# A selective-scan block and expert layer on one core: first state's tiles scaled by ScalarE, one of VectorE's sums kept back between two half scans, and the side work planned anew

## What is computed

```python
def step(h, inp):
    dAi, bxi, ci = inp            # exp(delta*A), delta*B*x, C
    h = dAi * h + bxi             # [b, 512, 16]
    return (h, jnp.einsum('ben,bn->be', h, ci))
...
y = jnp.transpose(ys, (1, 0, 2)) + Dp * x
return y * jax.nn.silu(z)
```

## Time and profile before

| | us |
|---|---|
| median of 3 runs (4428.97 to 4439.7) | 4429.01 |
| the profiled execution's own time | 4429.31 |
| its span | 4428.0 |
| VectorE busy (4736 instructions) | 3814.1, 86% |
| TensorE busy, matmuls | 3599.2, 81% |
| GpSimd busy | 3504.1, 79% |
| ScalarE busy | 3078.4, 70% |

### The profile page before, as it was taken

How to read it: one execution, slowest core, us unless ns; L and a number is a source line. 1 busy time by engine, 2 the same in 40 slices (tenths; PEclk the granted TensorE clock), 3 DMA queues, 4 the chain that set the end, 5 groups by cost and what they waited for, 6 DMA issues and landing times.

```text
span 4428.0 us, 57936 instructions
## 1 busy us (share of the span) xinstructions
PE 3599.2 (81%) x18192; PEld 2560.6 (58%) x18192; DVE 3814.1 (86%) x4736; ACT 3078.4 (70%) x5131; POOL 3504.1 (79%) x2085
## 2 busy tenths in 40 slices
PE   4668596888878888798978888888886988778877
PEld 1444454666556665567555774557654675557656
DVE  3999999998898989989898998989899898989710
ACT  4667576687767777678776886678776787668643
POOL 3898887988878888788887889878787888878611
PEclk7878697899979999899989998899997999889988
DMA  6222242557434674356543674346742575336555
GB/s 195 91 100 101 74 151 83 165 186 227 149 104 149 195 230 134 107 171 222 191 145 111 198 243 153 127 153 193 232 134 98 174 234 185 124 100 213 179 174 176
DMA packets 375804, 705.05 MB, mean 159 GB/s; under 512 B 31937, under 2 KB 205514, under 8 KB 371530
## 3 DMA queue, kind: packets, MB, share of 16 engines
q1 hardware_dynamic: 363210, 667.79, 46.3%
q0 software_dynamic: 12288, 33.57, 2.3%
HBM read 529.82 MB, written 171.44 MB: 158 GB/s over the span
## 4 chain that ended last, share of the span: by engine, by line
DVE 30%; PE 24%; POOL 15%; issue 15%; ACT 11%; DMA 3%; DVEq 0%; SPq 0%; POOLq 0%; ACTq 0%
DVE h L1391 12%; POOL drive L1895 8%; DVE h L1388 7%; DVE y L1405 7%; PE h_t L1165 5%; PE side L1199 4%; PE side L1336 3%; PE side L1328 3%; POOL xs_dram L1970 2%; ACT decay L1610 2%; POOL y L1913 2%; PE side L1227 1%; DMA expert_w<-in_w 1%; POOL drive L1901 1%; POOL work L1982 1%
## 5 line engine op out<-in xcount | busy, mean ns | idle before, releaser
L1895 POOL TENSOR_TENSOR drive<-xu,b_row 128x1024 f32<-128x1024 f32 x960 | 2261.8, 2361 | 396.7 <-DVE h L1391 237.7
L1610 ACT ACTIVATE decay<-delta,neg_a 128x512 f32<-128x512 f32 x2048 | 1400.8, 691 | 800.4 <-DVE h L1391 469.4
L1165 PE MATMUL h_t<-ident,h 128*128 128x128 f32 x8192 | 1339.5, 301 | 525.5 <-DVE y L1405 262.1
L1165 PEld LDWEIGHTS h_t<-ident,h 128*128 128x128 f32 x8192 | 1063.7, 155 | 992.0 <-DVE y L1405 381.7
L1405 DVE SCALAR_TENSOR_TENSOR y<-h_t,c_col,y 128x512 f32<-128x512 f32 x1488 | 1085.2, 729 | 76.3 <-PE h_t L1165 73.9
L1913 POOL TENSOR_TENSOR y<-y,scaled 128x512 f32<-128x512 f32 x496 | 631.4, 1273 | 120.7 <-ACT scaled L1631 119.5
L1391 DVE TENSOR_TENSOR_SCAN h<-decay,drive 128x512 f32<-128x512 f32 x512 | 621.8, 1214 | 64.6 <-ACT decay L1610 36.7
L1391 DVE TENSOR_TENSOR_SCAN h<-decay,h,drive 128x512 f32<-128x512 f32 x512 | 653.6, 1277 | 25.6 <-ACT decay L1610 8.0
L1388 DVE TENSOR_TENSOR_SCAN h<-decay,h,drive 128x512 f32<-128x512 f32 x448 | 572.8, 1279 | 53.2 <-ACT decay L1610 31.4
L1388 DVE TENSOR_TENSOR_SCAN h<-decay,drive 128x512 f32<-128x512 f32 x448 | 544.0, 1214 | 55.2 <-POOL drive L1895 48.5
L1199 PE MATMUL side<-prep_work,conv_diag 128*128 128x512 f32 x960 | 462.9, 607 | 24.2 <-DMA prep_work<-xz_dram 20.3
(11 more groups left out here) (206 smaller groups left out, 4343.8 us busy)
## 6 DMA issues: line engine op xcount, KB each, us to landing
expert_w<-in_w SPq DMA_DIRECT2D x350, 512.0 KB, 4.6
b_row<-b_dram SPq DMA_DIRECT2D x240, 512.0 KB
x_dram<-xu SPq DMA_DIRECT2D x16, 2048.0 KB, 7.6
delta_dram<-prep_work SPq DMA_DIRECT2D x64, 512.0 KB, 3.5
delta<-delta_dram SPq DMA_DIRECT2D x64, 512.0 KB, 4.4
ys_dram<-work SPq DMA_DIRECT2D x40, 512.0 KB, 6.2
work<-xs_dram SPq DMA_DIRECT2D x38, 512.0 KB, 4.9
h<-in_w SPq DMA_DIRECT2D x34, 512.0 KB
```

What stands on the lines that cost most here:

```text
L1165: t = pe.e.transpose(h_t[i % N_H_T][:, c * P:(c + 1) * P], its_h[:, c, :], ident[:, :])
L1610: act.e.activation(decay[:, i % N_DECAY, :], delta[:, c, its], ACT.Exp, scale=neg_a[:, c, w % 2, n:n + 1]).then_inc(decay_made, 1)
L1895: op = pool.e.tensor_tensor(drive[:, k % N_DRIVE, :], xu[:, w % 2, c, :], b_row[:, row % N_B_ROW, :], ALU.mult)
```

## The change

Three things.

1. All eight tiles of the first state of a sample's first direction (`is_first`) go to ScalarE, which scales them straight into `y`; VectorE's `tensor_scalar` is gone.
2. VectorE's sum of an odd tile whose next tile isn't VectorE's (`sum_is_late`) is kept back to the next step, where it stands behind the first half scan of the next unit. The order over four steps becomes: first half, sum, second half, first half, sum, second half, sum.
3. The tables `AT` and `BANK_USE` are other ones: the same 5048 pieces, in other steps and another order of the banks. Some of it: the second token load of sample 1 stands at 2848 (step 178) instead of 1712 (step 107); its four `u_mul` at steps 231 to 244 instead of 174 to 194; `slots` (the routing) of the seventh sample at step 1939 instead of 1916; the expert loads of sample 0, 46 from step 353 to 516 before, have the same ends and stand closer together in the middle; the last entry is step 2225 instead of 2232.

```diff
 AT = {
-    "tok_load": [-2240, -2239, 1456, 1712, 5216, 5600, 9153, 9648, ...
+    "tok_load": [-2240, -2239, 1456, 2848, 5232, 6561, 9202, 10800, ...
...
+        def is_first(i):
+            return i % (2 * TILES) < TB
+
         def by_pool(i):
-            return i % (2 * TB) in POOL_TILES
+            return i % (2 * TB) in POOL_TILES or is_first(i)
+
+        of_vector = list(accumulate(not by_pool(i) for i in range(NW * TILES)))
+        of_pool = list(accumulate(by_pool(i) and not is_first(i) for i in range(NW * TILES)))
 
         def summed_to(i):
-            rounds, into = divmod(i + 1, 2 * TB)
-            return rounds * (2 * TB - len(POOL_TILES)) + into - sum(t < into for t in POOL_TILES)
+            return of_vector[i]
...
         def gathered_to(i):
-            first_rounds, into = divmod(i, 2 * TILES)
-            in_first = [t for t in POOL_TILES if t < TB]
-            return pooled_to(i) - first_rounds * len(in_first) - sum(t <= into for t in in_first)
+            return of_pool[i]
...
+            def sum_is_late(i):
+                return i % 2 == 1 and i + 1 < NW * TILES and by_pool(i + 1)
+
             def sum_tile(i):
...
-                if d == 0 and n == 0:
-                    if b:
-                        dve.wait_ge(y_dumped[tb], 16 * b)
-                    dve.e.tensor_scalar(y[:, tb, :], h_t[i % N_H_T][:, :], c_n, None, ALU.mult).then_inc(summed, 1)
-                else:
-                    wait_y(dve, i)
-                    dve.e.scalar_tensor_tensor(...).then_inc(summed, 1)
+                wait_y(dve, i)
+                dve.e.scalar_tensor_tensor(...).then_inc(summed, 1)
...
                 i = s - 2 * EC
-                if 0 <= i < NW * TILES and not by_pool(i):
-                    sum_tile(i)
+                for its in (i - 1, i):
+                    if 0 <= its < NW * TILES and not by_pool(its) and sum_is_late(its) == (its < i):
+                        sum_tile(its)
...
             def scale_tile(i):
...
-                if d == 0 and n == 0:
+                if is_first(i):
...
-                if 0 <= i < NW * TILES and by_pool(i) and i % (2 * TILES) >= TB:
+                if 0 <= i < NW * TILES and by_pool(i) and not is_first(i):
                     pool_tile(i)
```

More of the change, by code:

```diff
@@ L2 @@
 from contextlib import ExitStack
+from itertools import accumulate
 import concourse.bass as bass
@@ L52 @@
[L52 to L58, removed]
@@ new lines @@
+    "tok_var": [-2160, -2128, 2736, 2912, 5808, 6656, 10352, 10864, 13762, 14240, 18672, 19184, 22017, 22448, 26113,
+        26960, 32992, 33073, 33457, 33584],
+    "neg_a": [-2144],
+    "tok_rstd": [-1952, -1920, 2752, 2928, 6464, 6656, 10720, 10880, 13760, 14368, 18976, 19200, 22016, 22656,
+        26112, 27232, 32992, 33072, 33456, 33584],
+    "tok_apply": [-1920, -1904, -1888, -1856, 2800, 2816, 2960, 2961, 6512, 6528, 6688, 6704, 10736, 10752, 10912,
+        10928, 13808, 13809, 14400, 14402, 19056, 19072, 19232, 19248, 22048, 22064, 22689, 22707, 26144, 26160,
+        27328, 27344, 33008, 33040, 33120, 33121, 33489, 33552, 33616, 33633],
@@ new lines @@
+    "xn_turn": [-1888, -1872, -1840, -1680, 2816, 2832, 2976, 2977, 6560, 6561, 6736, 6737, 10752, 10768, 10960,
+        10976, 13808, 13840, 14416, 14417, 19072, 19088, 19280, 19296, 22080, 22160, 22736, 22753, 26176, 26256,
+        27360, 27376],
+    "cw_make": [-1888, -1808, -1728, -1648, -1536, 160, 288, 416],
+    "xn_copy": [-1872, -1855, -1824, -1663, 2832, 2848, 2976, 2992, 6560, 6576, 6736, 6737, 10784, 10800, 10976,
+        10992, 13840, 13841, 14405, 14416, 19104, 19120, 19296, 19312, 22096, 22208, 22752, 22784, 26192, 26304,
+        27393, 27394],
@@ new lines @@
+    "silu_x": [-1551, -1328, 640, 3488, 4560, 7328, 8688, 11536, 12976, 15008, 17072, 19841, 21232, 23552, 25200,
+        27984, 29552],
+    "dbc_mm": [-1472, -1440, -1280, -1216, 688, 689, 720, 737, 3552, 3568, 3584, 3600, 4768, 4816, 4834, 4864, 7408,
[4 rows of a table added]
+    "dbc_copy": [-1408, -1168, 704, 768, 3616, 3632, 4784, 4880, 7456, 7504, 8752, 8801, 11680, 11696, 13008, 13136,
+        15152, 15536, 17105, 17184, 19984, 20016, 21296, 21424, 23696, 23760, 25266, 25376, 28112, 28304, 29600,
+        29664],
@@ new lines @@
+    "c_turn": [-1392, -1152, 784, 1120, 3680, 3681, 5200, 5201, 7568, 7664, 8850, 9008, 11792, 11808, 13216, 13232,
+        15505, 15905, 17249, 17312, 20064, 20112, 21440, 21473, 24224, 24240, 25408, 25425, 28258, 28384, 29728,
+        29792],
+    "c_copy": [-1376, -1120, 784, 1136, 3680, 3696, 5184, 5200, 7584, 7680, 8848, 9008, 11760, 11792, 13200, 13216,
+        15552, 15904, 17280, 17312, 20080, 20096, 21440, 21472, 24208, 24240, 25408, 25409, 28320, 28400, 29744,
+        29776],
+    "dt_mm": [-1376, -1168, -1120, -1104, -976, -960, -688, -656, 736, 800, 1168, 1184, 1248, 1249, 1344, 1360,
[8 rows of a table added]
@@ new lines @@
+    "softplus": [-1360, -1152, -1088, -1072, -944, -928, -16, 0, 752, 816, 1200, 1232, 1264, 1280, 1360, 1392, 3648,
[8 rows of a table added]
+    "delta": [-1328, -1120, -992, -991, 16, 17, 32, 33, 1120, 1136, 1216, 1248, 1296, 1312, 1376, 1408, 3664, 3680,
[7 rows of a table added]
+    "x_store": [-1280, 672, 3520, 4592, 7361, 8720, 11570, 12976, 15040, 17072, 19873, 21232, 23585, 25232, 28017,
+        29552],
+    "b_store": [-1168, 768, 3633, 4880, 7504, 8801, 11728, 13136, 15568, 17184, 20032, 21456, 23760, 25376, 28336,
+        29664],
@@ new lines @@
+    "top1": [5632, 10192, 14400, 18512, 22656, 26768, 30976, 33713],
+    "rank_mm": [5666, 10209, 14435, 18528, 22688, 26817, 31024, 33776],
+    "mix_turn": [5667, 5696, 10256, 10257, 14436, 14437, 18529, 18576, 22689, 22720, 26818, 26832, 31120, 31136,
+        33792, 33793],
+    "top2": [5648, 10208, 14416, 18528, 22672, 26784, 30992, 33744],
+    "slots": [5664, 10224, 14432, 18544, 22688, 26800, 31024, 33776],
+    "mix_copy": [5680, 5682, 10242, 10243, 14450, 14451, 18560, 18561, 22704, 22706, 26817, 26818, 31136, 31152,
+        33792, 33808],
@@ new lines @@
+    "bias_mm": [5856, 10448, 14992, 18688, 22896, 26960, 31104, 33856],
+    "bias_copy": [5856, 10434, 14992, 18720, 22914, 26992, 31120, 33888],
+    "xs_load": [5904, 5952, 6032, 6112, 6416, 6688, 10480, 10528, 10592, 10704, 11056, 11632, 14672, 14880, 14976,
+        15216, 15488, 15888, 18801, 18864, 18929, 19009, 19312, 19937, 22928, 22993, 23104, 23440, 23856, 24129,
+        27057, 27136, 27202, 27296, 27984, 28256, 31281, 31360, 31440, 31520, 31776, 32064, 34064, 34065, 34128,
+        34193, 34385, 34576],
@@ L431 @@
+    "fin_add": [9056, 9104, 9168, 9184, 13248, 13296, 13360, 13376, 17344, 17360, 17424, 17440, 21504, 21520, 21584,
+        21600, 25552, 25584, 25648, 25712, 29824, 29856, 29888, 29904, 33585, 33600, 33616, 33632, 35504, 35537,
+        35584, 35600],
+    "out_store": [9201, 13393, 17457, 21617, 25729, 29921, 33648, 35552, 35600],
 }
 BANK_USE = {
[L434 to L435 removed]
@@ new lines @@
+    "z_mm": [72, 73, 79, 84, 103, 106, 105, 108, 248, 251, 250, 253, 273, 272, 275, 274, 400, 402, 407, 404, 428,
+        429, 430, 431, 555, 564, 557, 566, 577, 592, 579, 594, 713, 715, 716, 717, 738, 743, 740, 745, 878, 873,
+        880, 875, 898, 895, 900, 897, 1019, 1036, 1021, 1038, 1041, 1064, 1043, 1066, 1078, 1080, 1059, 1082, 1061,
+        1084, 1063, 1073],
+    "y_turn": [91, 96, 95, 100, 110, 114, 113, 118, 265, 264, 267, 266, 277, 276, 279, 278, 417, 420, 422, 421, 432,
+        433, 434, 435, 567, 582, 584, 571, 581, 596, 583, 598, 730, 735, 732, 737, 742, 747, 744, 749, 890, 887,
+        892, 889, 902, 899, 904, 901, 1052, 1033, 1035, 1056, 1045, 1068, 1047, 1070, 1109, 1113, 1136, 1123, 1162,
+        1143, 1168, 1151],
@@ new lines @@
+    "rank_mm": [140, 296, 459, 616, 769, 921, 1096, 1175],
+    "mix_turn": [143, 145, 299, 301, 460, 462, 603, 605, 766, 768, 926, 928, 1100, 1079, 1198, 1200],
+    "eo_mm": [147, 142, 148, 155, 298, 303, 309, 306, 465, 469, 488, 487, 607, 618, 624, 615, 770, 772, 793, 797,
+        930, 923, 929, 938, 1075, 1098, 1106, 1085, 1163, 1190, 1204, 1179],
+    "bias_mm": [153, 304, 485, 613, 781, 936, 1077, 1177],
+    "xs_turn": [150, 157, 154, 156, 160, 163, 168, 171, 178, 181, 206, 210, 311, 308, 310, 315, 319, 316, 331, 330,
[19 rows of a table added]
@@ L506 @@
+    "comb_mm": [240, 243, 245, 249, 397, 399, 396, 398, 554, 556, 551, 553, 705, 710, 709, 711, 861, 863, 865, 876,
+        1026, 1013, 1030, 1017, 1174, 1176, 1178, 1161, 1229, 1252, 1231, 1254],
+    "tok_apply": [1158, 1160, 1182, 1184],
 }
@@ L1069, in wait_tile @@
                 engine.wait_ge(summed, summed_to(before))
-            elif before % (2 * TILES) < TB:
+            elif is_first(before):
                 engine.wait_ge(tile_scaled, pooled_to(before))
```

228 lines of the change are left out of this document (85 added, 143 removed), and 615 rows, old and new, of tables (AT, BANK_USE).

## The result

The changed kernel takes 4442.0 us (median of 15 runs) against 4433.3 for the kernel before in the same comparison: ratio 1.0022, 95% interval 1.0015 to 1.0030. That is some 10 us slower, where 61 us less was forecast. It lies inside the 0.3% that I called no change, on the slower side, and outside the range of 4322 to 4412.

What follows compares the result with a forecast made beforehand. VectorE was taken to bound the state loop outside its 7% of true waits. Gains of 58 and 11 us less 8 made 61, taking 4429.3 to 4368 us, with a range of 4322 to 4412.

Steps and rivals of the forecast that it cites:

- For the rest VectorE sets the pace: State loop: some 300 us, 7%, are true waits of VectorE; in the remaining time VectorE decides the speed.
- A sum between the halves: VectorE's dependent half scans: a kept-back sum between them saves 0.19 us at each of 373 bare pairs, 70.9 us.
- Rival D: VectorE's scan pairs: the 0.19 us goes with any two scans in a row and only moves; 4419 us, chance 0.06.
- the share: VectorE's 67.9 us given up by the pairs counts at 0.85, so 58 us arrive.
- So I cost it at nothing.: TensorE's transposition of tile i+3: its PSUM buffer is released 1.13 us later, covered by slack, cost nothing.
- My slack of 2.2 us: Time TensorE has left before the sum of tile i+3 needs its transposed tile, some 2.2 us.
- rival E: TensorE's late transposition holds up side matmuls and VectorE: 4510 us, chance 0.05; sign: VectorE's tile waits at 150 us or more.
- I bound it at a tenth of them either way, +-30 us, and take 0.: New side-work tables: they can reshuffle VectorE's 300 us of waits, by at most 30 us either way; taken as 0.
- First states: First-state scalings moved from VectorE to ScalarE: between nothing and 21 us gained, 11 taken.
- The y dumps: ScalarE's first-state scaling waits for dumps of all eight tiles: cost nothing, at most 14 us if cover is gone.
- The sum: Whole kernel: 58 us by pairs plus 11 from first states less 8 behind late drives, 61 us gained.
- B: Rival: another engine takes over in the loop, only a third of 79 us arrives; 4403, up to 4415 us, chance 0.17.

Runs made afterwards that it cites:

- the narrow sum: Kernel before, order and tables unchanged, but every fourth tile's second sum adds only 384 of 512 columns to y: 4397.6 us, ratio 0.9934.
- pool_tile_1: Kernel before with its old tables, but GpSimd's tile is the second of each four, not the third: 4487.2 us, ratio 1.0130.
- pool_tile_3: Kernel before with its old tables, but GpSimd's tile is the fourth of each four, not the third: 4494.9 us, ratio 1.0147.

## Why the prediction was wrong

**What bounds the kernel.** VectorE is the busiest engine and its spacings were read rightly. "For the rest VectorE sets the pace" went too far. I took every us in which VectorE didn't wait as its own; the narrow sum shows that only 44 of 100 us taken from it arrive. An engine that is 92% busy isn't thereby the bound for 92% of the time. With the narrow sum, VectorE's waits for tiles went from 73.9 to 81.5 us and those for decays from 82.9 to 98.7. (I also called TensorE the nearest rival, though GpSimd is the busier one in the loop, 3416 to 3359 us.)

**A sum between the halves.** The 0.19 and the 373 pairs held: 28 bare pairs are left and the cycle is 6.54. On the question of the pipeline flush (the Trainium skill, "VectorE: DVE Perf Modes", section "The DRAIN you can't avoid") the page's rule that a semaphore costs nothing extra doesn't hold for this pair: two independent scans stand 1.18 apart in the changed kernel, the dependent pair 1.32. The second half both waits on the semaphore and needs the first's last column, and no run parts the two. Rival D falls. The value of the 68 us was mis-sized by the share: 0.44, so about 30 us and not 58.

**"So I cost it at nothing."** This step, the later release, failed for the old tables: 58 us where I had nothing. My slack of 2.2 us was worked out for a cycle in which TensorE has only transpositions to do. But it has side work near nine tenths of the kept-back sums (450 of 503, from the step before its own to three steps after), and the gating piece above alone takes 1.98 + 1.05 us at the full clock. What the runs showed in place of the nothing: TensorE's wait for these sums rose by 84 us, its side matmuls queued behind, and VectorE waited for their results and for decays. I had priced just this in rival E at 1.13 x 126 = 142 us and gave it 0.05, on the ground that TensorE "is mostly ahead". But an average says little of the places that count. Tile by tile, 101 of those us are at the 223 tiles with no TensorE side piece within two steps, and only 21 at the 859 tiles with such pieces in four or all five of these steps.

**"I bound it at a tenth of them either way, +-30 us, and take 0."** This is the step that decided the result. The tables alone cost 66 us, twice the bound. I named three moves as examples, but nearly nine in ten of the 5048 entries stand a step or more from where they were, by 7 steps in the median. I held them for a shuffle of work that VectorE's waits limit to 300 us in all; but they decide those waits, and a uniform shift by one step costs 127. Their effect also can't be added to the rest: the kept-back sum costs 58 us with one table and gains 34 to 47 with the other.

**First states.** 11 us expected; 0 on the old tables, 9 (66 to 57) and 22 (32 to 10) on the new, each uncertain by some 8 to 10. The y dumps cost nothing, as costed: they land in 2.0 to 7.6 us, and no scaling of ScalarE waits for one.

**The sum.** 58 + 11 - 8 = 61 by my terms; measured with the new tables under it, the edits give 56. That is nearly luck: the kept-back sum gave 34 of it and the first states 22, where I had 50 and 11, and the share that I used is twice the one measured on the old tables. Whether it is nearer my value on the new ones wasn't tried. What is missing is the + 66 for the tables. -56 + 66 = +10.

**The rivals.** B came nearest in its signs (unused time up by 65 us, over three sources), but with 4403 instead of 4442. E's waits for tiles, 117.6 us, stayed under the 150 I had set. Even in the kept-back sum alone, where the late release costs 58 us, they are 102.1: most of the damage shows as waits for decays and side results, so my sign for E was the wrong one. TensorE's own wait for VectorE's sums would have told.

**What stays open.** What in the new tables costs the 66 us with the old order, and why with the new order they don't reach what the old ones reach on theirs. I varied the tables only as a whole and by a shift; which rows of them cost the time wasn't tried. Nor is it shown why pool_tile_1 and pool_tile_3 lose 58 and 65 us: they move ScalarE's and GpSimd's step on the tile. The shift experiment shows that one step can cost as much, but it moved all side work, and no kernel took that apart. How much the lower TensorE clock adds isn't shown either.

## What to carry to other kernels

In a program whose side work is placed by hand among the steps of a loop, any move of one step, even one that shortens the busiest engine, must be priced with its placement: here moving all side work by one step and nothing else cost 2.9%, and the new placement alone 1.5%. Before forecasting from an engine's busy share, measure what its time is worth, by shortening an instruction and leaving everything else in place. And apply a reordering only where the queue behind it is empty: 160 of 503 places gave -0.4% where all of them gave +1.3%.

## What I had not expected of the hardware

The same matmuls took 3.62 us instead of 1.98 and 1.91 instead of 1.05, at a granted clock of 0.52 instead of 1.00, in a stretch where TensorE had stood idle 1.3 to 2.3 us at a time. Both kernels lose the clock there: the windows read 0.67 over 5 us in the kernel before, and 0.70, 0.50 and 0.52 over 15 us with the kept-back sum. So most of a wait for TensorE's result (here some 2.5 of 3.9 us, the estimate above) can be the clock and not the queue. A row of waits doesn't tell: read the clock of the window beside it.
